# A selective-scan kernel on one core: layer-norm statistics on ScalarE, half of the output gates on ScalarE and GpSimd

## What is computed

```
xs, z = split(x @ in_w)                     # 512 + 512 channels
xc    = silu(conv4(xs) + cb)
dt, B, C = split(xc @ xp_w)
delta = softplus(dt @ dt_w + dt_b)
h     = h * exp(delta * A) + (delta * xc) * B      # per token, 512 channels x 16 states
y     = sum over states of h * C + xc * D_skip
out   = (y * silu(z)) @ out_w               # y * silu(z) is the gate
x     = layer_norm(out + x) * ln_w + ln_b
```

## Time and profile before

| | |
|---|---|
| median of three runs | 8305.31 us (8304.15 to 8310.86) |
| the profiled execution | 8300.88 us, its span 8299.1 us |
| DVE busy | 7941.7 us, 96% |
| POOL busy | 6969.2 us, 84% |
| PE busy | 6477.3 us, 78% |
| ACT busy | 5386.9 us, 65% |
| scan turns | about 155 to 7570 us |
| feed-forward layer | about 7606 to the end |

### The profile page before, as it was taken

The page is one execution under the profiler, slowest core; times in us unless marked ns, Lnnn a source line. Parts: engine busy times, 40 slices in busy tenths (PEclk is TensorE's granted clock), DMA queues, the critical chain, the costliest instruction groups (busy, mean ns, idle before and its releaser), DMA issues. The chain is left out here.

```text
span 8299.1 us, 74989 instructions
## 1 busy us (share of the span) xinstructions
PE 6477.3 (78%) x21028; PEld 2508.4 (30%) x21028; DVE 7941.7 (96%) x7922; ACT 5386.9 (65%) x8693; POOL 6969.2 (84%) x3380
## 2 busy tenths in 40 slices
PE   5778777777877777777777777777777777775888
PEld 2222222222222222222222222222222222222555
DVE  8999999999999999999999999999999999996777
ACT  5666676666666776667766667667666667663444
POOL 3898889988898888988899888988889888885555
PEclk8999999999999999999999999999999999987999
DMA  6444454444554454544544445454555445441110
GB/s 181 118 117 108 106 125 117 117 115 113 126 120 109 101 118 117 121 120 108 125 117 117 104 110 125 117 127 103 117 120 120 110 103 120 117 115 55 38 38 30
DMA packets 566552, 909.74 MB, mean 110 GB/s; under 512 B 58384, under 2 KB 200720, under 8 KB 564880
## 3 DMA queue, kind: packets, MB, share of 16 engines
q1 hardware_dynamic: 566160, 905.25, 45.5%
HBM read 716.08 MB, written 188.94 MB: 109 GB/s over the span
## 5 line engine op out<-in xcount | busy, mean ns | idle before, releaser
L890 POOL TENSOR_TENSOR hc<-h,crep 128x1024 f32<-128x1024 f32 x2048 | 4783.1, 2359 | 760.6 <-PE acc L473 672.7
L1009 DVE TENSOR_TENSOR_SCAN h<-dA,carry,bu 128x512 f32<-128x512 f32 x3072 | 3762.3, 1263 | 8.4 <-POOL hc L890 8.4
L628 ACT ACTIVATE dA<-drep,cur 128x512 f32<-128x512 f32 x4096 | 2618.1, 710 | 4.8 <-DMA drep<-delta_dram 3.5
L994 DVE TENSOR_TENSOR bu<-durep,B_all 128x1024 f32<-128x1024 f32 x2048 | 2477.2, 1210 | 97.4 <-PE B_all L455 63.3
L455 PE MATMUL B_all<-dtc,spread_b 128*128 128x512 f32 x2048 | 1326.8, 734 | 1556.3 <-DVE bu L994 1555.2
L637 ACT COPY carry<-h 128x4 f32<-128x4 f32 x1023 | 201.3, 197 | 2117.5 <-DVE h L1009 2115.9
L473 PE MATMUL acc<-hc,gather 128*32 128x512 f32 x8192 | 1273.1, 697 | 4.1 <-POOL hc L890 4.1
L1009 DVE TENSOR_TENSOR_SCAN h<-dA,bu 128x512 f32<-128x512 f32 x1024 | 1194.2, 1201 | 6.8 <-POOL hc L890 3.4
L497 PE MATMUL work<-xT,inw 128*128 128x512 f32 x2048 | 1027.9, 648 | 69.9 <-ACT xT L648 59.1
L455 PEld LDWEIGHTS B_all<-dtc,spread_b 128*128 128x128 f32 x2048 | 361.3, 209 | 2243.3 <-DVE bu L994 2182.8
L507 PE MATMUL work<-xs,taps 128*128 128x512 f32 x2048 | 957.1, 610 | 0.0
(11 more groups left out here) (176 smaller groups left out, 6667.3 us busy)
## 6 DMA issues: line engine op xcount, KB each, us to landing
drep<-delta_dram SPq DMA_DIRECT2D x1024, 256.0 KB, 6.0
durep<-du_dram SPq DMA_DIRECT2D x1024, 256.0 KB, 6.7
crep<-c_dram SPq DMA_DIRECT2D x1024, 64.0 KB, 6.4
delta_dram<-za SPq DMA_DIRECT2D x64, 1024.0 KB, 4.2
du_dram<-relu SPq DMA_DIRECT2D x64, 1024.0 KB, 5.3
x_in<-xbuf SPq DMA_DIRECT2D x64, 512.0 KB, 3.8
x_res<-xbuf SPq DMA_DIRECT2D x64, 512.0 KB, 3.8
xbuf<-x_res SPq DMA_DIRECT2D x64, 512.0 KB, 5.5
```

Source lines behind the costliest of these rows:

```text
L628: act.activation(dA[:, 4 * (s % 2) + k, :], drep[q % 2][:, k, :], ACT.Exp, scale=cur[:, p_, 4 * s + k:4 * s + k + 1]).then_inc(da_ready, 1)
L890: pool.tensor_tensor(hc[:, pair, :], h[:, pair, :], crep[:, j:j + 1, :].to_broadcast([P, 2, T]), ALU.mult).then_inc(hc_ready, 1)
L994: dve.tensor_tensor(bu[:, 2 * k:2 * k + 2, :], durep[q % 2][:, 2 * k:2 * k + 2, :], B_all[:].unsqueeze(1).to_broadcast([P, 2, T]), ALU.mul ...
L1009: dve.tensor_tensor_scan(h[:, r, :], dA[:, r, :], bu[:, k, :], start, ALU.mult, ALU.add).then_inc(scanned, 1)
```

## The change

- The buffer `x_in` is dropped. The x of chunk n is loaded into the first half of `xc[:, n % 2]`, which is free once block 1's skip term of chunk n-2 has been summed; `load_x(g + 2)` now stands ahead of `load_delta(g, ., 3)` in the same turn. The space is used for a new tile `sums` of two banks' size.
- `statistics` and `moments` on DVE are gone. `copy_out` is done in four pieces of 128x256 with a row sum as accumulator output; POOL's new `mean` (step 8) makes the negative mean from them; ACT's new `squares` (step 9) squares x_res minus mean into `sums`, with the row sum of squares as accumulator output; POOL's `variance` scales and adds eps in two dependent operations.
- The gates of block 1 (step 10) and block 3 (step 2 of the next turn) leave DVE. ACT copies acc into `sums` (`take_sums`, between `keep_states` and `exp` of that step), which frees acc; POOL multiplies it with sz (`gate`, behind `times_c` of that step). The gates of blocks 0 and 2 (steps 6 and 14) stay on DVE. PE's `project_out` waits for `gated` too.

The diff, with declarations of semaphores and tiles left out:

```diff
@@ sync
             def load_x(n):
                 c = ready(n % CH)
-                if positive(n):
-                    sp.wait_ge(w_filled[1], fill(1, n - 1, "tr") + 1)
-                sp.dma_start(x_in[:], xv[c]).then_inc(x_loaded, 16)
+                if n >= 2:
+                    sp.wait_ge(summed, 2 * (NG * (n - 2) + QS) + 1)
+                sp.dma_start(x_in[n % 2], xv[c]).then_inc(x_loaded, 16)
...
                     store_c(n, p_)
+                if not is_last(g) and not (isinstance(g, int) and g == TOT - 2):
+                    load_x(g + 2)
                 load_delta(g, 1 - p_, 3)
...
                         at_layer(g + 2, (ph + 2) % 4, load_mid)
-                        load_x(g + 3)
@@ tensor
             def project_out(m, p_, j):
                 if j == 0:
+                    pe.wait_ge(gated, 2 * (m + 1))
                     pe.wait_ge(acc_read, DB * (m + 1))
@@ scalar
             def copy_out(m, j):
                 wait_filled(act, j, out_fill(j, m))
-                act.copy(x_res[:, 2 * j:2 * j + 2, :], W[j][:].rearrange("p (t d) -> p t d", t=2)).then_inc(w_read[j], 1)
+                for t in range(2):
+                    act.activation(x_res[:, 2 * j + t, :], W[j][:, t * D:(t + 1) * D], ACT.Identity,
+                                   accum_out=row_sum[:, 2 * j + t:2 * j + t + 1]).then_inc(w_read[j] if t else row_summed, 1)
+
+            def take_sums(n, q):
+                act.wait_ge(summed, 2 * (NG * n + QS * (q + 1)))
+                if positive(2 * n + q // 2):
+                    act.wait_ge(gated, 2 * n + q // 2)
+                squares_ahead = n if q == 1 else min(n, TOT - 1)
+                if positive(squares_ahead):
+                    act.wait_ge(squared, squares_ahead)
+                act.copy(sums[:, 0, :], acc[:]).then_inc(acc_read, 1)
+
+            def squares(m):
+                act.wait_ge(mean_ready, m + 1)
+                act.wait_ge(gated, 2 * m + 2)
+                if positive(m):
+                    act.wait_ge(squared, m)
+                for t in range(NT):
+                    ins = act.activation(sums[:, t // 2, t % 2 * D:(t % 2 + 1) * D], x_res[:, t, :], ACT.Square, bias=minus_mean[:, t:t + 1],
+                                         accum_out=sq_sum[:, t:t + 1])
+                ins.then_inc(squared, 1)
...
                     keep_states(group(g, s - 1))
+                    if s == 2 and not is_first(g):
+                        take_sums(g - 1, DB - 1)
+                    if s == 10:
+                        take_sums(g, 1)
                     exp(group(g, s + 1), here if s + 1 < NG else other)
...
                     if not is_first(g):
+                        if s == 9:
+                            squares(g - 1)
                         if s == 11:
                             root_guess(g - 1)
@@ gpsimd
+            def gate(n, p_, q):
+                if q == 1:
+                    pool.wait_ge(z_done, n + 1)
+                pool.wait_ge(acc_read, DB * n + q + 1)
+                pool.tensor_tensor(sz[:, p_, q, :], sums[:, 0, :], sz[:, p_, q, :], ALU.mult).then_inc(gated, 1)
...
+            def mean(m):
+                for j in range(2):
+                    pool.wait_ge(w_read[j], out_fill(j, m) + 1)
+                pool.tensor_tensor(minus_mean[:], row_sum[:], c_minus[:], ALU.mult).then_inc(mean_ready, 1)
+
             def variance(m):
-                pool.wait_ge(means, m + 1)
-                pool.tensor_tensor(ve[:], mv[:, :, 1], c_eps[:], ALU.add).then_inc(var_ready, 1)
-                pool.tensor_tensor(minus_mean[:], mv[:, :, 0], c_minus[:], ALU.mult)
+                pool.wait_ge(squared, m + 1)
+                pool.tensor_tensor(ve[:], sq_sum[:], c_over[:], ALU.mult).then_inc(newton, 1)
+                pool.wait_ge(newton, 6 * m + 1)
+                pool.tensor_tensor(ve[:], ve[:], c_eps[:], ALU.add).then_inc(var_ready, 1)
                 pool.wait_ge(var_ready, m + 1)
                 pool.tensor_tensor(half_ve[:], ve[:], c_half[:], ALU.mult).then_inc(newton, 1)
...
                     times_c(group(g, s))
+                    if s == 2 and not is_first(g):
+                        gate(g - 1, other, DB - 1)
+                    if s == 10:
+                        gate(g, 1 - other, 1)
                     if not is_first(g):
+                        if s == 8:
+                            mean(g - 1)
                         if s == 10:
                             variance(g - 1)
@@ vector
-            def statistics(m):
-                for j in range(2):
-                    dve.wait_ge(w_read[j], out_fill(j, m) + 1)
-                for t in range(NT):
-                    ins = dve.bn_stats(st[:, t], x_res[:, t])
-                ins.then_inc(stats, 1)
-
-            def moments():
-                for t in range(NT):
-                    ins = dve.bn_aggr(mv[:, t], st[:, t])
-                ins.then_inc(means, 1)
...
                     scan(at, ph, 0)
-                    if s == 2 and not is_first(g):
-                        gate(g - 1, other, DB - 1)
-                    if s in (6, 10, 14):
+                    if s in (6, 14):
                         gate(g, here, (s - 6) // 4)
...
-                    if s == 9 and not is_first(g):
-                        dve.wait_ge(stats, g)
                     scan(at, ph, 3)
-                    if not is_first(g):
-                        if s == 8:
-                            statistics(g - 1)
-                        if s == 9:
-                            moments()
```

More of the change, by code:

```diff
@@ L105, in mamba_layers @@
         xc = sb("xc", [P, 2, DB, T])
+        x_in = [xc[:, i, 0:2].rearrange("p e t -> p (e t)").rearrange("p (t d) -> p t d", t=NT) for i in range(2)]
+        sums = sb("sums", [P, 2, T])
         sz = sb("sz", [P, 2, DB, T])
@@ L128, in mamba_layers @@
         carry = sb("carry", [P, NA])
-        st, mv = sb("stats", [P, NT, 6]), sb("mv", [P, NT, 2])
+        row_sum, sq_sum = sb("row_sum", [P, NT]), sb("sq_sum", [P, NT])
         ve, half_ve, minus_mean, lnv, guess, tmp, root, shift = (
             sb(n, [P, NT]) for n in ("ve", "half_ve", "minus_mean", "lnv", "guess", "tmp", "root", "shift"))
-        c_eps, c_half, c_minus, c_three = (sb(n, [P, NT]) for n in ("c_eps", "c_half", "c_minus", "c_three"))
+        c_eps, c_half, c_over, c_minus, c_three = (sb(n, [P, NT]) for n in ("c_eps", "c_half", "c_over", "c_minus", "c_three"))
         c_dram = nc.dram_tensor("c_dram", (2, 4 * QS, T), F32, kind="Internal").ap()
@@ L157, in mamba_layers @@
             sem(n) for n in ("da_ready", "bb_ready", "bu_ready", "scanned", "hc_ready", "summed", "carried"))
-        acc_read, stats, means, var_ready, lnv_done, guess_ready, newton, root_done, normed, weighted, x_ready = (
-            sem(n) for n in ("acc_read", "stats", "means", "var_ready", "lnv_done", "guess_ready", "newton",
+        acc_read, gated, row_summed, mean_ready, squared, var_ready, lnv_done, guess_ready, newton, root_done, normed, weighted, x_ready = (
+            sem(n) for n in ("acc_read", "gated", "row_summed", "mean_ready", "squared", "var_ready", "lnv_done", "guess_ready", "newton",
                              "root_done", "normed", "weighted", "x_ready"))
@@ L439, in _ @@
             store_x(TOT - 1)
-            sp.wait_ge(x_loaded, 16 * TOT)
+            sp.wait_ge(x_loaded, 16 * (TOT - 1))
             sp.wait_ge(x_stored, 16 * TOT)
@@ L482, in transpose_x @@
                     pe.wait_ge(n0_normed, 1)
-                src = x_in if positive(n) else spot(0)
+                src = x_in[n % 2] if positive(n) else spot(0)
                 for d in range(KD):
@@ L870, in _ @@
             turns(act, turn)
+            take_sums(TOT - 1, DB - 1)
             for j in range(2):
                 copy_out(TOT - 1, j)
+            squares(TOT - 1)
             root_guess(TOT - 1)
@@ L923, in newton_step @@
                 pool.tensor_tensor(tmp[:], guess[:], guess[:], ALU.mult).then_inc(newton, 1)
-                pool.wait_ge(newton, 5 * m + 2)
+                pool.wait_ge(newton, 6 * m + 3)
                 pool.tensor_tensor(tmp[:], tmp[:], half_ve[:], ALU.mult).then_inc(newton, 1)
-                pool.wait_ge(newton, 5 * m + 3)
+                pool.wait_ge(newton, 6 * m + 4)
                 pool.tensor_tensor(tmp[:], c_three[:], tmp[:], ALU.subtract).then_inc(newton, 1)
-                pool.wait_ge(newton, 5 * m + 4)
+                pool.wait_ge(newton, 6 * m + 5)
                 pool.tensor_tensor(root[:], tmp[:], guess[:], ALU.mult).then_inc(newton, 1)
-                pool.wait_ge(newton, 5 * m + 5)
+                pool.wait_ge(newton, 6 * m + 6)
                 pool.tensor_tensor(shift[:], minus_mean[:], root[:], ALU.mult).then_inc(root_done, 1)
@@ L974, in _ @@
             turns(pool, turn)
+            gate(TOT - 1, 1, DB - 1)
+            mean(TOT - 1)
             variance(TOT - 1)
@@ L1051, in _ @@
```

(16 more changed lines are left out.)

2 lines of the change are left out of this document (removed).

## The result

The changed kernel takes 8496.19 us (median of four runs, 8489.64 to 8503.05), the kernel before in the same comparison 8304.73 us. The ratio is 1.0229 with a 95% interval from 1.0217 to 1.0241: 191 us slower, where 97 were forecast, and 6 us outside the range, on its upper side.

A forecast was written before the change was run, and what follows sets the result against it. A loop through ACT, POOL, du's DRAM trip, PE and DVE was taken as the bound: 115.75 - 0.33 + 1.63 + 0.61 = 117.66 a turn, +1.56 for 62 turns, +97 us, 8400 us; range 8290 to 8490.

The forecast's parts named there:

- the loop: Way through ACT, POOL's softplus, du via DRAM, ACT's step 1, PE and DVE: 115.75 us a turn, against DVE's work 115.1.
- POOL's leg: Softplus start to du product's end on POOL: gate, mean and variance add 1.63, a 0.33 wait goes; net +1.30.
- The late acc: Step 2: ACT's copy frees acc later than DVE's gate did, delaying PE's skip matmul; +0.61, bounds 0 and 2.
- the two PE legs: Skip to x projection, 3.22, and x projection to DVE's product for step 4, 4.65; both left unchanged in the sum.
- Rival A: The forecast itself: the loop at 116.8 to 118.6 a turn, 8345 to 8460 us; chance 0.58.
- Rival D: Step 11: PE's in-projection at the lower clock takes 3.5 more, delaying B for step 13; 119.4 a turn, 8508 us; chance 0.13.
- The stalls' places: DVE's new waits a turn: about 2.7 at step 14 (or 13), 0.9 for durep at step 0, 1.7 at step 4.
- The rest of ACT's load: Squares 2.1, second acc copy 0.47, copy_out perhaps 0.9 more, accumulator outputs 0 to 0.3 each; hidden in ACT's idle time.
- The x load: SP's load of x goes to another place; delta for step 12 queued behind it is needed much later; no effect.
- B: Rival: DVE alone is the bound and its freed time comes out, 174 us less, 8131; chance 0.08.
- C: Rival: no change, as PE catches up at the upper clock and late acc costs nothing; 116.1 a turn, 8290 to 8320; chance 0.14.
- the du leg: du's end on POOL through DRAM to DVE's first product of the next turn; taken as fixed at 15.40.

The follow-up runs named there:

- e4: The kernel before with only the statistics moved to ACT and POOL, all four gates staying on DVE: 8292.31 us, ratio 0.9989.
- e2: The changed kernel with the gate of block 3 (step 2) put back on DVE: 8378.47 us, ratio 1.0092.
- e6: The changed kernel with ACT's copy of acc for block 3 moved into step 1, ahead of silu_z and its table load: 8347.72 us, ratio 1.0055.
- e7: e6 with POOL's gate of block 1 moved from step 10 to step 3 of the next turn: 8278.86 us, ratio 0.9971.
- e9: e7 with POOL's variance (and its followers) moved behind the last softplus product and POOL's affine products moved to step 2: 8216.94 us, ratio 0.9898.
- e10: The changed kernel with one extra, unread PE matmul at step 2 between B broadcast and skip: 8424.04 us, ratio 1.0144.
- e1: The changed kernel with ACT's root_guess at step 11 put behind the two xT copies: 8490.42 us, ratio 1.0226.

## Why the prediction was right in its way and wrong in its size

**The bound.** Right. DVE's 96% was no bound: e4 took 94 us of DVE's work away for 9 us of time, and the change took 173 away and lost 191. But the argument for the loop was weaker than it read: "The sum is 115.75, just that turn's length" holds for any set of legs laid end to end. What shows the loop is that shortening one leg shortens the turn, in e2, e6, e7 and e9. One leg was also read wrongly. The forecast has ACT's table load between DVE's first product and PE's skip matmul; its own row of the B pair, [5.42 <-DVE bu L994] in the earlier trace rows, names DVE's product, and e6 starts skip during that table load. In the kernel before, the table load's end and the B pair's only happened to fall together.

**POOL's leg.** Right: 43.28 forecast, 43.26 measured. The gate, interpolated between 723 and 2359 ns to 1270, took 1276. The waits of POOL for PE at step 10 are gone. e7 shows that the gate's place, not the gate, is its price. Against the mean turn before the leg grew by 0.91, as POOL's wait for PE at step 10 was 0.72 on average and not the 0.33 of the turn in the earlier trace rows. The rule that the prediction weighed against the row (the Trainium skill, GPSIMD Engine Reference, section 4.1 Engine selection), twice VectorE's time, would have given 1.33; the measured 1276 ns against 666 on DVE is 1.92 times.

**The late acc.** Right in place and nearly in size as far as the start of skip goes: +0.61 forecast, +0.81 measured against the mean turn. Its 0.06 for the semaphore had no row; from the copy's end to skip's start are 0.14 in every turn of after. Against e6, where acc is in time, the copy's place costs 1.41.

**The step that failed** is the size of the term for the late acc and PE behind it. It is +0.61 in the sum, with "Bounds: 0 if PE's matmuls catch up, and 2 if the added idle keeps PE at the lower clock". I named the upper end and then took the added time on PE as nothing: the sum has 3.22 and 4.65 for the two PE legs, as if the clock were not touched, and no reason is given. They measured 3.82 and 5.47, together 1.42 a turn, 88 of the 94 us between 8402 and 8496. With the 0.81 the whole term is 2.23, above even the upper bound. Rival A's 116.8 to 118.6 does not hold that bound either: 117.66 - 0.61 + 2 is 119.05 a turn, some 8488 us. The rows spoke for the upper end: the B pair at 4098.54 already ran at 1.2 GHz after 5.42 of idle time, and the change puts another pause right behind it. e10 shows the mechanism: with acc as late as in the change, but no pause, the two legs are 2.72 and 4.65 (before 3.20 and 4.67), and the x projection takes 3.70 in every turn. The Trainium skill (TensorE: Matmul & The Clock Gate, Part 1) says that an idle TensorE falls to 1.2 GHz and stays there a while after work starts. The trace agrees at step 2 too, with a granted clock of 0.50 from 4087.1 to 4096.0 behind 4.83 of idle time; I had used the page at step 11 and not at step 2, where it counts.

**Rival D**, whose time was nearest, was wrong as a cause: its stall is there (3.7 a turn, between the 1.7 of the forecast and the 5.2 that D's B at 4060.9 gives), and taking it away (e1) gains 6 us in 8490, no more than the spread. The input projection was 1.8 longer and not 3.5, and so the chain ended about together with du's. In e10, where it is 2.6 longer, the chain does cost time.

**The stalls' places.** At step 4 DVE waits 3.4 a turn, where 1.7 was forecast; the clock's 1.42 is most of the difference. The 2.7 forecast for step 14 (or 13) stood at step 13's product (3.7), and durep's 0.9 came out as 0.25. **The rest of ACT's load**: hidden, as forecast. copy_out in four pieces with the reads of the accumulator adds 0.5 rather than 0.9, squares take 1.98 with their reads instead of 2.1 without. **The x load**: no leg shows it, but no run had it alone; every kernel from after on loads x in the new way.

**Rivals B and C**: no run is near B's 8131. C needed acc in time; e6 has acc in time and is 8348, with a turn of 116.88: POOL's leg is 0.88 longer than before and the leg to skip only 0.60 shorter. So C was too hopeful by 0.8 a turn.

## What to carry to other kernels

Follow a turn round from an instruction to the same instruction a turn later, leg by leg; where two such ways are within 1% of each other, busy shares say nothing, and work belongs where the loop waits, even if it is on a fuller engine. The place in its queue of a copy that frees a bank matters: behind the silu and its table load it cost 2.4 us a turn more than ahead of them (119.30 against 116.88). And where a wait is added right behind a longer idle time of PE, charge the following matmuls at the lower clock. The legs of a turn always add up to it, so a loop is shown as the bound only when a changed leg changes the turn; and the largest stall in a profile may be free, so take it away once before building on it.

## What the runs showed of the hardware

- ACT's accumulator output is an instruction of its own behind the activation. Rows of after, by group:

```profile
L756 ACT ACTIVATE sums<-x_res,minus_mean 128x256 f32<-128x256 f32 x256 | 127.1, 498 | 116.4 <-POOL minus_mean L954 116.4
...
L756 ACT ACTIVATION_READ_ACCUMULATOR sums<-x_res,minus_mean 128x1 f32 x256 | 48.0, 188 | 0.0
```

  188 ns long, and 0.09 from its start to the next one's, so eight of them cost about 0.7 us of ACT's time a turn. The squares with one pointer operand take 498 ns; normalise, with two and the same shape, took 589. They differ in function too, and no run parts the two.
- A pause of 1.09 us of PE at the 1.2 GHz level, behind an idle stretch of 4.83, left the following sums and nearly half of the x projection at that level (1.94 and 4.82); a matmul of no use in its place brought them to 1.19 and 3.70 and the kernel 72 us ahead. Without a pause the sums still vary from turn to turn between 1.07 and 1.94 (e6), so one turn alone tells little; the averages are 1.91 and 4.52 with the pause, 1.56 and 3.75 in e6, 1.23 and 3.70 in e10. How the lower level's length hangs on the pause was not tried.
- Why the du leg varies between 15.6 and 15.9 from kernel to kernel was not tried either; it accounts for half of e2's miss.
